# Channel mixing in a four-layer convolution stack: load ring of channel pairs, loads and product stores on one queue, masks made inside the mixing block, one mixing block per layer

## Reference, cut to what matters

```python
x = x + L0(gn(x)); x = x + L1(gn(x)); x = x + L2(gn(x)); x = x + L3(gn(x))
L0: z = einsum('bikc,bkjc->bijc', a, b)                 # 16 channels
L1: h = h * mask[..., None]; a1, b1, a2, b2 = split(h, 4)
    x1 = einsum('bikd,bjkd->bijd', a1, b1)              # 16 channels
    x2 = einsum('bkid,bkjd->bijd', a2, b2)              # 16 channels
L2: tri = einsum('bikc,bjkc->bijc', a, b)               # 64 channels
L3: left, right = (.. ) * m[i] * m[k]
    out = einsum('bkid,bkjd->bijd', left, right)        # 64 channels
```

## Time and profile before

| what | us |
|---|---|
| three runs, median (lowest, highest) | 1714.95 (1713.91, 1717.31) |
| the profiled execution | 1716.62 |
| its span | 1714.7 |

### The profile page before, as it was taken

One profiled execution on the slowest core, in us unless ns is written; L12 is line 12 of the kernel. 1 busy time (PEld: TensorE's weight loads), 2 busy tenths in 40 slices (PEclk: granted clock), 3 DMA queues, 4 the chain that ended last, 5 costly groups with the idle time before them and its releaser, 6 DMA issues. The chain is left out here.

```text
span 1714.7 us, 26817 instructions
## 1 busy us (share of the span) xinstructions
PE 1435.4 (84%) x9119; PEld 750.9 (44%) x9119; DVE 1172.3 (68%) x2060; ACT 1050.5 (61%) x1845; POOL 429.0 (25%) x382
## 2 busy tenths in 40 slices
PE   5796697968587697899979997998899967785987
PEld 5535432212376242133338996222233336663443
DVE  5643587179688884289957777893499956677664
ACT  4674686844234786688856666556688834444555
POOL 5400197130000594310000000792500000000665
PEclk9898899989898898999989998998899989997999
DMA  8336310026657230079987886891088878785998
GB/s 341 105 153 225 143 54 9 1 87 194 213 205 278 99 99 13 1 270 345 344 315 298 302 302 235 303 378 51 26 343 341 345 272 319 305 305 198 375 393 314
DMA packets 140872, 381.51 MB, mean 222 GB/s; under 512 B 13505, under 2 KB 13634, under 8 KB 130626
## 3 DMA queue, kind: packets, MB, share of 16 engines
q1 hardware_dynamic: 118418, 314.95, 50.4%
q10 hardware_dynamic: 22320, 64.86, 10.1%
HBM read 191.01 MB, written 188.74 MB: 221 GB/s over the span
## 5 line engine op out<-in xcount | busy, mean ns | idle before, releaser
L1350 POOL TENSOR_TENSOR xT<-xT,work 128x512 f32<-128x512 f32 x192 | 241.7, 1277 | 700.6 <-DVE work L1395 698.2
L1046 PE MATMUL bank<-work 128*128 128x256 f32 x1408 | 349.3, 401 | 59.4 <-DVE work L1112 23.9
L746 ACT ACTIVATE work<-bank,bias 128x512 f32<-128x512 f32 x448 | 286.1, 686 | 96.3 <-PE bank L645 42.0
L1046 PEld LDWEIGHTS bank<-work 128*128 128x128 f32 x1408 | 277.7, 205 | 104.5 <-DMA work<-hidden_rows 31.9
L645 PE MATMUL bank<-work,w 64*64 64x512 f32 x2048 | 257.2, 605 | 6.0 <-ACT work L742 6.0
L818 DVE SCALAR_TENSOR_TENSOR work<-bank,bias,work 128x512 f32<-128x512 f32 x320 | 236.4, 748 | 31.8 <-PE bank L645 24.2
L1069 ACT COPY work<-bank 128x512 f32<-128x512 f32 x176 | 103.3, 587 | 235.9 <-PE bank L1046 182.7
L1534 POOL TENSOR_TENSOR xT<-xT,work 128x512 f32<-128x512 f32 x64 | 80.2, 1275 | 384.4 <-ACT work L1504 384.4
L1138 DVE TENSOR_TENSOR work<-work 128x512 f32<-128x512 f32 x176 | 121.1, 688 | 71.9 <-ACT work L1069 70.5
L1395 DVE SCALAR_TENSOR_TENSOR work<-bank,bias,work 128x512 f32<-128x512 f32 x192 | 141.9, 748 | 38.2 <-ACT work L1325 22.8
L645 PEld LDWEIGHTS bank<-work,w 64*64 64x64 f32 x2048 | 84.4, 134 | 141.5 <-DVE work L818 83.0
(11 more groups left out here) (149 smaller groups left out, 2084.2 us busy)
## 6 DMA issues: line engine op xcount, KB each, us to landing
hidden_rows<-work SPq DMA_DIRECT2D x128, 512.0 KB, 3.8
work<-hidden_rows SPq DMA_DIRECT2D x60, 1024.0 KB, 7.8
products<-work ACTq DMA_DIRECT2D x88, 512.0 KB, 4.9
work<-products SPq DMA_DIRECT2D x88, 512.0 KB, 4.6
work<-gate_rows SPq DMA_DIRECT2D x64, 512.0 KB, 5.5
work<-hidden SPq DMA_DIRECT2D x18, 1024.0 KB, 8.2
work<-in_x SPq DMA_DIRECT2D x32, 512.0 KB, 4.8
gate_rows<-work SPq DMA_DIRECT2D x32, 512.0 KB, 2.7
```

The source lines that it names most:

```text
L746: nc.scalar.activation(result(t, column), GB[n % len(GB)][:, :], ACT.Sigmoid, bias=bias(name)).then_inc(gate_sb, 1)
L1046: mm = pe.matmul(ZB[c % 2][:, r * N:r * N + N], a[:, kk, rows_of(r)], x[:, kk, :], start=(kk == 0), stop=(kk == 1))
L1350: pool.tensor_tensor(columns(t), columns(t), term[:, t % RING, :], ALU.add).then_inc(x_sb, 1)
```

## The change

- `mix` is called once for each layer. Layer 1's two parts become one loop of 32 channels, of which the first `turned` = 16 are turned and the others masked and not turned.
- `ab` (same size) becomes a ring of `RING` = 4 pairs of channels for each operand. The first two pairs are loaded channel by channel (four singles per operand), operand 0 by SP and operand 1 by ACT. Pairs 2 and 3 are loaded at once behind them, and pair g+4 when pair g has been multiplied and copied. A pair load is 512 KB per operand. The refill waits for the copies of pair g in all layers, since SP waits for `z_sb` and stores before it loads.
- The product stores move from ACT to SP, in this order for each pair: wait for the copies of pair g, store pair g, load pair g+4.
- `zs` holds `OUT` pairs: 3, 2, 3, 4 in layers 0 to 3 (it was 2 in all).
- `make_mask` goes. ACT issues the mask loads at the head of `mix`, before it waits for the rows of `project`. In layer 1 TensorE's transposes and VectorE's copy follow. In layer 3 the row of the mask is loaded with a broadcast to 128 partitions, and no matmul spreads it.
- `project0` and `project` return their stores' semaphores, and SP and ACT wait for them in `mix`, instead of SP at the end of `project`.
- `finish` (layer 2) and `finish_out` issue the first three gate loads before they wait for the products.

```diff
-            for b, s in enumerate(stored):
-                sp.wait_ge(s, 16 * len(range(b, PAIRS // 2, OUT)))
+    return [(s, 16 * len(range(b, PAIRS // 2, OUT))) for b, s in enumerate(stored)]
...
-            for s in range(RP):
-                sp.wait_ge(stored[s], 16 * stores * len(range(s, PAIRS, RP)))
-def make_mask(core, layer, mask, mask_t):
...
-def mix(core, layer, part, channels, offsets, turns, z_row, cz, mask, mask_t, sums):
+    return [(stored[s], 16 * stores * len(range(s, PAIRS, RP))) for s in range(RP)]
+
+
+def mix(core, layer, channels, offsets, turned, turns, cz, rows_out, mask, mask_t, sums):
...
-    LOAD = 4
+    SINGLES, RING = 4, 4
+    OUT = {0: 3, 1: 2, 2: 3, 3: 4}[layer]
     X = 2 * N
...
-    zs, at = core.area([4, X], 4 * X)
-    ab, at = core.area([4 * LOAD, X], at)
+    zs, at = core.area([2 * OUT, X], (2 if mask is None else 4) * X)
+    ab, at = core.area([4 * RING, X], at)
...
+    turns_of = lambda c: turns if c < turned else (False, False)
+    masked_load = lambda c: layer == 1 and c >= turned
+
+    def source(o, c, n):
+        first = offsets[c >= turned][o] + (c - turned if c >= turned else c)
+        return image[:, :, :, first:first + n, :].rearrange("w v h m x -> (v h) w (m x)")
...
+        def wait_rows(eng):
+            for s, n in rows_out:
+                eng.wait_ge(s, n)
+
+        def load_single(eng, o, c):
+            eng.dma_start(places(o, c, 1).rearrange("p m x -> p (m x)"), source(o, c, 1)).then_inc(single[c], 16)
 
         @block.sync
         def _(sp):
-            for c in range(LOAD):
+            def load(g):
                 for o in range(2):
-                    sp.dma_start(to_source(slots(o, 0)[:, c:c + 1, :]), source(offsets[o] + c, 1)).then_inc(single[c], 16)
-            for g in range(1, channels // LOAD):
-
-                if nturn == 2:
-                    at_least(sp, turn_mm, 2 * LOAD * (g - 1))
-                else:
-                    at_least(sp, z_mm, LOAD * (g - 1))
-                for o in range(2):
-                    first = offsets[o] + g * LOAD
-                    sp.dma_start(to_source(slots(o, g)), source(first, LOAD)).then_inc(landed[g % 2], 16)
-            if layer == 1 and part == 0:
-                for s in stored:
-                    sp.wait_ge(s, 16 * (channels // 4))
+                    sp.dma_start(places(o, 2 * g, 2).rearrange("p m x -> p (m x)"),
+                                 source(o, 2 * g, 2)).then_inc(landed[g % RING], 16)
+
+            def store(g):
+                sp.wait_ge(z_sb, 2 * g + 2)
+                sp.dma_start(zdst[:, :, :, 2 * g:2 * g + 2, :].rearrange("w v h c x -> (v h) w (c x)"),
+                             zs[:, 2 * (g % OUT):2 * (g % OUT) + 2, :].rearrange("p c x -> p (c x)")
+                             ).then_inc(stored[g % OUT], 16)
+
+            wait_rows(sp)
+            for c in range(SINGLES):
+                load_single(sp, 0, c)
+            for g in range(SINGLES // 2, RING):
+                load(g)
+            for g in range(PAIRS):
+                store(g)
+                if g + RING < PAIRS:
+                    sp.wait_ge(z_mm, 2 * g + 2)
+                    load(g + RING)
...
+            if layer == 1:
+                pe.wait_ge(mask_in, 16)
+                for kk in range(2):
+                    for r in range(2):
+                        mm = pe.transpose(MB[:, kk * N + r * P:kk * N + r * P + P], mask[:, r, kk * P:kk * P + P],
+                                          core.ident[:, :])
+                mm.then_inc(mask_mm, 1)
...
                 if c % 2 == 0:
-                    at_least(act, stored[c // 2 % 2], 16 * (c // 4))
-                at_least(act, s1_sb, c - 3)
-                nc.scalar.copy(zs[:, c % 4, :], ZB[c % 2][:, :]).then_inc(z_sb, 1)
+                    at_least(act, stored[c // 2 % OUT], 16 * (c // 2 // OUT))
+                at_least(act, s1_sb, c - 2 * OUT + 1)
+                nc.scalar.copy(zs[:, c % (2 * OUT), :], ZB[c % 2][:, :]).then_inc(z_sb, 1)
...
+            if layer == 1:
+                act.dma_start(mask, core.ins["L1_conv_mask"].rearrange("a (p e) k -> p (a e) k", e=2)).then_inc(mask_in, 16)
+            if layer == 3:
+                m = core.ins["L3_conv_src_mask"]
+                act.dma_start(mcol, m.rearrange("a (p e) -> p (a e)", e=2)).then_inc(mask_in, 16)
+                act.dma_start(columns_mask, m.broadcast_to([P, N])).then_inc(mask_in, 16)
+            wait_rows(act)
+            for c in range(SINGLES):
+                load_single(act, 1, c)
             for c in range(channels):
...
+            if layer == 1:
+                dve.wait_ge(mask_mm, 1)
+                dve.tensor_copy(mask_t, MB[:, :]).then_inc(mask_sb, 1)
+                dve.wait_ge(mask_sb, 1)
+            if layer == 3:
+                dve.wait_ge(mask_in, 32)
+                dve.tensor_tensor(msq, mcol, mcol, ALU.mult).then_inc(mask_sb, 1)
+                for k in range(2):
+                    dve.tensor_scalar(mask[:, k, :], columns_mask, mcol[:, k:k + 1], None, ALU.mult).then_inc(mask_sb, 1)
+                dve.wait_ge(mask_sb, 1)
...
+            if stored_gate:
+                for i in range(IN):
+                    load_gates(i)
             for s, n in products_out:
                 sp.wait_ge(s, n)
...
-        make_mask(core, 1, mask, mask_t)
-        mix(core, 1, 0, 16, (0, 16), (True, True), 0, 32, mask, mask_t, sums)
-        out = mix(core, 1, 1, 16, (32, 48), (False, False), 16, 32, mask, mask_t, sums)
+        out = mix(core, 1, 32, [(0, 16), (32, 48)], 16, (True, True), 32, rows, mask, mask_t, sums)
```

More of the change, by code:

```diff
@@ L935, in mix @@
     shift, msq = core.fold[:, 11:12], core.fold[:, 8:10]
-    LOAD = 4
+    SINGLES, RING = 4, 4
+    OUT = {0: 3, 1: 2, 2: 3, 3: 4}[layer]
     X = 2 * N
-    nturn = sum(turns)
-    masked_turn, masked_load, row_mask = layer == 1 and nturn == 2, layer == 1 and nturn == 0, layer == 3
-    zs, at = core.area([4, X], 4 * X)
-    ab, at = core.area([4 * LOAD, X], at)
+    PAIRS = channels // 2
+    masked_turn = layer == 1
+    row_mask = layer == 3
+    zs, at = core.area([2 * OUT, X], (2 if mask is None else 4) * X)
@@ L953, in mix @@
     TB = [[bank[0], bank[1]], [bank[2], bank[3]]]
     ZB = [bank[4], bank[5]]
[L956 to L961 removed]
+    MB = bank[6]
@@ new lines, in mix @@
+    nturn = sum(turns)
+    turns_of = lambda c: turns if c < turned else (False, False)
[3 more added lines that the diff above has]
+        return image[:, :, :, first:first + n, :].rearrange("w v h m x -> (v h) w (m x)")
+    with ExitStack() as ctx:
+        (mask_in, mask_mm, mask_sb, masked_a, masked_b, turn_mm, ta_sb, tb_sb, z_mm, z_sb, sq_sb, s1_sb, s2_sb, begun,
+         shifted) = core.sems(f"mix{layer}", "mask_in mask_mm mask_sb masked_a masked_b turn_mm ta_sb tb_sb z_mm z_sb "
+                              "sq_sb s1_sb s2_sb begun shifted")
+        single = core.sems(f"mix{layer}", " ".join(f"single{c}" for c in range(SINGLES)))
+        landed = core.sems(f"mix{layer}", " ".join(f"in{n}" for n in range(RING)))
+        stored = core.sems(f"mix{layer}", " ".join(f"st{n}" for n in range(OUT)))
@@ L1057, in _, with turned_a @@
         def _(act):
-            def turned(c):
-                if turns[0] and not masked_turn:
+            def turned_a(c):
+                if turns_of(c)[0] and not masked_turn:
                     act.wait_ge(turn_mm, nturn * c + 1)
@@ L1155, in _ @@
             summed(channels - 1)
-    return [(s, 16 * (channels // 4)) for s in stored]
+    return [(s, 16 * len(range(n, PAIRS, OUT))) for n, s in enumerate(stored)]
 class Roots:
```

127 lines of the change are left out of this document (58 added, 69 removed).

## The result

The changed kernel takes 1640.3 us, median of four runs, beside 1714.4 for the kernel before. The ratio is 0.958, with a 95% interval of 0.954 to 0.961: faster. The forecast was 1638.5, in a range of 1628 to 1662.

A forecast was written before the change was run, and what follows sets the result against it. It saw layer 2 bound by TensorE and layer 3 by load waits, its DMA engines idle between bursts. Terms 41 + 4.8 + 5.4 + 13.3 + 9.9 + 1.1 + 1.0 = 76.5 us gave 1638.5, range 1628 to 1662.

The forecast's parts named there:

- Layer 3, steady: Layer 3's mixing loop: the DMA engines become the bound at 3.82 us a pair, a gain of 41 us.
- The rule weighed against it: Layer 3's loads: the skill's 341 GB/s at 1 MB would make a pair 4.6 us, the gain 22.
- The stores on the load queue: Product stores behind up to three pairs of loads: put at 0, though a wait may remain at layer 1's copy.
- Layer 0, steady: Layer 0's mixing: copies 2.19 us apart without the two load stalls, a gain of 9.9 us.
- Layer 1, one block: Layer 1's two parts in one loop: masked channels follow directly on VectorE, a gain of 13.3 us.
- Layer 3, start: Layer 3's start: mask loaded beside the stores, 4.2 us, and issue by two engines, 0.6; a gain of 4.8.
- Layer 1, start: Layer 1's start: the same as layer 3's, a gain of 5.4 us, or 3 if the mask's load ends last.
- Layers 0 and 2, start: Starts of layers 0 and 2: first operands or channels sooner, gains of 1.1 and 1.0 us.
- Lower rate: Rival, layer 3: mixed half-size loads and stores on one queue give 340 to 370 GB/s; 1655 us, chance 0.14.
- Latency: Rival, layer 3: load latency sets the ring's pace, 18.5 us for four pairs; gain 22, whole 1657, chance 0.11.
- Dead time: Rival, shared queue: dead time between store and next load makes it slower, deciding at 0.56 us a DMA; chance 0.04.
- Not doing what it says: Rival: layer 3's pauses come from something other than late release; only block terms, 35 us, remain: 1680, chance 0.02.

The follow-up runs named there:

- the ring of three: The changed kernel with a ring of three pairs instead of four: 1683.7 us, ratio to the kernel before 0.980 to 0.987.
- both edits: The changed kernel, slots refilled only after every second pair and pairs used only once their neighbour has landed too: 1780.5 us, ratio 1.036 to 1.043.

## Why the prediction was right

**Layer 3, steady.** Predicted 41, measured 40.1. The steps held: the DMA engines became the bound, a pair takes 3.75 us (3.82 predicted) at 419 GB/s (412 predicted), VectorE's waits for loads split into pieces of at most 3.2 us, stores keep no copy waiting. One term inside was mis-sized: the loop of four pairs is not 12 us but about 13.7, from the ring of three. So 3.4 us a pair stands against 3.75, and the margin that lets the queue stay filled is 0.3 us a pair and not 0.8. The text had taken the shortest landing of before, 5.1 us; with the queue full the median is 7.7. The term was right because the bound was another resource; with three pairs the same estimate missed by a factor of four, 43 us instead of 5 to 15.

**The rule weighed against it.** With 512 KB loads and stores mixed, layer 3 moves 419 GB/s for 80 us, and 409 with loads of 256 KB. The Trainium skill (DMA: Bandwidth & Descriptors, Rules for kernel authors) wants at least 1 MiB in a DMA, and the same page's measured table, of DMAs issued from GpSimd, has 341 GB/s for 1 MB; by that rate the whole would have been 1658. The trace does not agree where DMAs queue up behind one another.

**The stores on the load queue.** Put at 0 where four buffers cover them: right. With two buffers the price in layer 3 is 8 us. In layer 1, which has two, one wait of 0.7 us is left at the copy, beside a full VectorE.

**Layer 0, steady.** Predicted 9.9, measured 9.8. All products after the first take 1.89 us but one (1.99), and copies come 2.19 us apart without a stall; the first lines of it:

```profile
146.96 0.60 ACT L1044 COPY work<-bank 128x512 f32<-128x512 f32 x1
149.15 0.58 ACT L1044 COPY work<-bank 128x512 f32<-128x512 f32 x1 [0.53 <-PE bank L1014]
151.34 0.59 ACT L1044 COPY work<-bank 128x512 f32<-128x512 f32 x1 [0.54 <-PE bank L1014]
```

**Layer 1, one block.** Predicted 13.3, measured 13.9. VectorE goes from turned to masked channels without a gap; the masks of the second part (L1078) are made between the turns of the first:

```profile
484.79 0.69 DVE L1113 TENSOR_TENSOR work<-work 128x512 f32<-128x512 f32 x1
485.39 1.29 DVE L1078 TENSOR_TENSOR work<-work 128x512 f32<-128x512 f32 x2
486.59 1.28 DVE L1097 TENSOR_TENSOR work<-bank,work 128x512 f32<-128x512 f32 x2
```

**Layer 3, start.** Predicted 4.8, measured 5.6; 3.6 of it comes from the masks, and the prediction's 0.6 for issue by two engines is not there. The 2.0 that are left were not taken apart.

**Layer 1, start.** Predicted 5.4, measured 2.9 in one execution and 5.3 in another. The step that was missing is the clock of the first product, for which the text had no case. Its case of 3 us, a mask load that ends last, is not what happened, though the 2.9 looks like it: the mask had landed at 442.02 and the first turn (443.47) waited for the first channel.

**Layers 0 and 2, start.** 1.1 and 1.0 predicted. Layer 0's first copy comes 9.1 to 11.0 us after its first load instead of 11.2, a gain of 0.2 to 2.1. In layer 2 no gain can be told from the variation.

**The finishes.** 0, as said; the 3.2 us by which the stretch looked longer are variation.

**The rivals.** Lower rate: 419 GB/s says no. Latency: the loop is 13.7 us and not 18.5; but this rival was nearer than it looked. Dead time: 0.04 us a DMA, against the 0.56 from which it would decide. Not doing what it says: undoing the ring's grain gives layer 3's time back. The 35 us that this case had left over held layer 0's 9.9, which hang on the ring too (44.7 us in layer 0 with both edits).

**The sum.** The three steady terms carry it, 64.2 predicted and 63.8 measured. The starts were to give 12.3 us; of the 70.5 between the two profiled executions only 6.7 are left for them and all the rest, and of the 74.7 between the kernel before and the other execution of the changed kernel about 10. That the median came within 1.8 us of the forecast is in part luck of the executions.

No version that was run is faster than the changed kernel. Layer 3's mixing is now bound by bytes, layer 1's by VectorE, layer 2's by TensorE.

## What to carry to other kernels

Before making loads larger, write down the loop of a buffer: release, issue, landing, the compute up to the next release. Divide it by the buffers in the ring and compare with the time of the stage's bound. Refilling and waiting in small units shortens the loop twice, at the same storage, and here 512 KB and even 256 KB loads kept the rate. Price that loop with the landing time under load and leave a margin: one pair less cost 43 us.

Look at what the releasing instruction stands behind in its engine's order. A release by an instruction that comes after a look-ahead wait for the next data takes that data's latency into the loop; release at the last reader ahead of it.

Compare a stage in two or three executions before explaining 3 us of it.

## What the runs showed of the hardware

One queue with loads and stores in turn filled the DMA engines as well as two (419 and 415 GB/s, shares 1.02 on one, 0.68 + 0.34 on two), and 256 KB DMAs gave 409. A store's landing time was the same on either queue.

TensorE came into layer 1's mixing after about the same idle time, 8 us, in twelve executions and was granted its upper level in five by the start of the first product, in seven later (1.89 to 1.96 against 2.66 to 3.62 us for the same eight matmuls).
